# Neighbourhood attention: projections one step sooner, three input blocks on chip, the second block's keys copied apart from its queries

## The reference

```python
qkv = (x @ qkv_w + qkv_b).reshape(B, H, W, 3, HEADS, HEAD_DIM)
q = qkv[..., 0, :, :] * HEAD_DIM ** (-0.5)
kwin = kk[:, idx_h[:, None, :, None], idx_w[None, :, None, :]]      # 7 x 7 keys of each token
vwin = v[:, idx_h[:, None, :, None], idx_w[None, :, None, :]]
scores = jnp.einsum('bxyhd,bxyklhd->bxyhkl', q, kwin) + bias[None]
attn = jax.nn.softmax(scores.reshape(B, H, W, HEADS, k * k), axis=-1)
out = jnp.einsum('bxyhkl,bxyklhd->bxyhd', attn, vwin).reshape(B, H, W, C)
attn_out = out @ proj_w + proj_b
gate = sigmoid(relu(x @ g1_w + g1_b) @ g2_w + g2_b)
return attn_out * gate + x
```

## Time and profile before

| | us |
|---|---|
| median of 3 runs | 4253.98 |
| the profiled execution's own time | 4251.54 |
| its span, from the first to the last instruction | 4249.4 |
| PE busy in it | 3954.3 (93%) |
| DVE busy | 3166.3 (75%) |
| ACT busy | 2744.4 (65%) |
| POOL busy | 1219.7 (29%) |

### The profile page before, as it was taken

How to read it: one execution, slowest core, us unless ns; L and a number is a source line. 1 busy time by engine, 2 the same in 40 slices (tenths; PEclk the granted TensorE clock), 3 DMA queues, 4 the chain that set the end, 5 groups by cost and what they waited for, 6 DMA issues and landing times. The chain is left out here.

```text
span 4249.4 us, 73556 instructions
## 1 busy us (share of the span) xinstructions
PE 3954.3 (93%) x25466; PEld 3038.4 (72%) x25466; DVE 3166.3 (75%) x7667; ACT 2744.4 (65%) x6175; POOL 1219.7 (29%) x1283
## 2 busy tenths in 40 slices
PE   7899997899999999999999999978799987889899
PEld 5677776699988989889988899966566642333247
DVE  5777776677787777877778777759466668887775
ACT  4667766677777777767777667649434447776643
POOL 2444443100011000110001000015124448886753
PEclk8899998899999999999999999999899985887789
DMA  6655554000011000100001000032233345554446
GB/s 176 167 153 158 155 153 114 4 26 21 21 31 33 18 26 16 36 29 23 21 19 42 15 11 9 11 87 75 91 135 119 114 147 180 173 170 154 145 158 208
DMA packets 284396, 365.84 MB, mean 86 GB/s; under 512 B 38650, under 2 KB 169722, under 8 KB 283258
## 3 DMA queue, kind: packets, MB, share of 16 engines
q1 hardware_dynamic: 270154, 343.83, 26.7%
q0 software_dynamic: 12288, 16.92, 1.4%
q10 hardware_dynamic: 1584, 0.40, 0.0%
HBM read 192.80 MB, written 115.34 MB: 73 GB/s over the span
## 5 line engine op out<-in xcount | busy, mean ns | idle before, releaser
L911 ACT ACTIVATE l_ph<-l_T 128x512 fp32r<-128x512 f32 x1024 | 611.8, 597 | 549.2 <-PE l_T L816 549.2
L1028 DVE TENSOR_TENSOR l_pl<-l_T,l_ph 128x512 fp32r<-128x512 f32 x1024 | 707.2, 691 | 275.1 <-ACT l_ph L911 274.4
L1017 DVE CUSTOM_DVE_ANT_0 l_pr<-l_S,l_zero 128x512 f32<-128x512 f32 x1024 | 704.6, 688 | 75.1 <-PE l_S L739 12.1
L916 ACT ACTIVATE l_pr<-l_pr,l_st 128x512 f32<-128x512 f32 x1024 | 731.4, 714 | 1.1 <-DVE l_st L1023 1.0
L828 PE MATMUL l_O<-l_ph,l_vh 128*128 128x256 f32 x2048 | 661.8, 323 | 12.1 <-DVE l_pl L1028 12.0
L816 PE MATMUL l_T<-l_ident,l_pr 128*128 128x128 f32 x4096 | 613.0, 272 | 0.0
L816 PEld LDWEIGHTS l_T<-l_ident,l_pr 128*128 128x128 f32 x4096 | 507.8, 140 | 136.2 <-issue 0.2
L829 PE MATMUL l_O<-l_ph,l_vl 128*128 128x256 f32 x2048 | 577.9, 282 | 0.0
L830 PE MATMUL l_O<-l_pl,l_vh 128*128 128x256 f32 x2048 | 576.2, 281 | 0.0
L1060 POOL TENSOR_TENSOR l_xs<-l_xs,l_bob 128x128 f32<-128x128 f32 x128 | 57.2, 459 | 1643.1 <-DMA l_xs<-x 1641.7
L737 PE MATMUL l_S<-l_kh,l_qh 128*128 128x512 f32 x1024 | 417.6, 408 | 0.3 <-DVE l_kl L977 0.2
(11 more groups left out here) (259 smaller groups left out, 8235.0 us busy)
## 6 DMA issues: line engine op xcount, KB each, us to landing
l3b_u<-ub SPq DMA_DIRECT2D x128, 512.0 KB, 4.0
l_kq<-l_hl SPq DMA_DIRECT2D x384, 128.0 KB, 3.2
zs<-l_tmp SPq DMA_DIRECT2D x64, 256.0 KB, 2.2
ub<-l3a_u SPq DMA_DIRECT2D x32, 512.0 KB, 3.2
l3b_z<-zs SPq DMA_DIRECT2D x64, 256.0 KB, 3.6
yz<-l3b_z SPq DMA_DIRECT2D x64, 256.0 KB, 3.2
l3b_dt<-yz SPq DMA_DIRECT2D x32, 512.0 KB, 4.2
l_vg<-vs SPq DMA_DIRECT2D x256, 55.0 KB
```

The costliest lines, as they stand in the source:

```text
L911: e.activation(ph[:, i, :], psT[:, i, :], ACT.Copy).then_inc(p_hi, 1)
L916: e.activation(pr[:, s, es], pr[:, s, es], ACT.Exp, bias=st[:, s, 9:10], scale=SC, accum_out=st[:, s, 10 + k:11 + k]).then_inc(exped, 1)
L1017: e.tensor_tensor_reduce(pr[:, s, ks], psS[:, bk, :], zero[:].broadcast_to([128, 512]), 1.0, -3.0e38, ALU.add, ALU.max, st[:, s, kc:kc + 1 ...
L1028: e.tensor_tensor(pl[:, i, :], psT[:, i, :], f32(ph[:, i, :]), ALU.subtract).then_inc(p_lo, 1)
```

## The change

The jobs of each block are done one step sooner: step 4(G-2)-1 for "k", then "q", "v" and "hide" in 4(G-2) to 4(G-2)+2. For this `xn` gets a third slot and its semaphores, and ("k", 2) joins the list ahead of the loop. `stack` can copy keys or queries alone: for block 1 the 12 key copies stay where they were, and 12 further copies of its queries, with a semaphore of their own (`q1_in`), stand behind the stores of the first values; scores of block 1 wait for both. The bias classes 3 to 5 are loaded in step 1 instead of 2, and 6 to 8 one each in the steps 14, 18 and 22 instead of together in step 12. The last two pieces of the diff are the wait of PE ahead of the scores of block 1 and that of ACT before it writes `hl` again for block 3.

```diff
-        xn = P.sb("xn", [128, 2, 512])
+        xn = P.sb("xn", [128, 3, 512])
...
+        q1_in = P.sem("q1_in")
...
         def jobs(n):
-            G, i = n // 4 + 2, n % 4
+            G, i = (n + 1) // 4 + 2, (n + 1) % 4
             return [(("k", "q", "v", "hide")[i], G)] if G < NB else []
...
-        before = [("q", 0), ("k", 0), ("k", 1), ("v", 0), ("q", 1), ("v", 1), ("hide", 0), ("open", 0), ("hide", 1), ("open", 1)]
+        before = [("q", 0), ("k", 0), ("k", 1), ("v", 0), ("q", 1), ("v", 1), ("hide", 0), ("open", 0), ("hide", 1), ("open", 1), ("k", 2)]
...
             def fetch(G):
-                s, sl = G % 2, slice(512 * rb, 512 * rb + 512)
-                if G >= 2:
+                s, sl = G % 3, slice(512 * rb, 512 * rb + 512)
+                if G >= 3:
                     for what in ("k", "q", "v", "hide"):
-                        full(w, (what, G - 2))
+                        full(w, (what, G - 3))
...
-            def stack(G):
+            def stack(G, what=("q", "k"), landed=None):
-                for what in ("q", "k"):
-                    emptied(w, (what, G))
+                for x in what:
+                    emptied(w, (x, G))
...
+                to = slice(q_at if "q" in what else k_at, k_at + 1 if "k" in what else q_at + 1, k_at - q_at)
                 for h in range(4):
                     hs = slice(32 * h, 32 * h + 32)
-                    for k, which in enumerate((slice(0, 3, 2), slice(1, 3), slice(0, 4, 3))):
-                        e.dma_start(f32(kq[32 * k:32 * k + 32, h, q_at:k_at + 1:k_at - q_at, :]), f32(halves[hs, which, :])).then_inc(kq_in[G % 4], 16)
+                    for k, (q_part, k_part) in enumerate(((0, 2), (1, 2), (0, 3))):
+                        part = slice(q_part if "q" in what else k_part, k_part + 1 if "k" in what else q_part + 1, k_part - q_part)
+                        e.dma_start(f32(kq[32 * k:32 * k + 32, h, to, :]), f32(halves[hs, part, :])).then_inc(landed or kq_in[G % 4], 16)
...
-            fetch(0)
-            fetch(1)
+            for G in range(3):
+                fetch(G)
...
             stack(0)
-            stack(1)
-            fetch(2)
+            stack(1, ("k",))
             keep_v(0)
             keep_v(1)
+            stack(1, ("q",), q1_in)
             fetch(3)
...
-                if n == 2:
+                if n == 1:
                     for k in range(3, 6):
                         bias(k)
-                elif n == 12:
-                    for k in range(6, 9):
-                        bias(k)
+                elif n in (14, 18, 22):
+                    bias(6 + (n - 14) // 4)
...
+                if G == 1:
+                    w.wait_ge(q1_in, 192)
...
+                    if G == 3:
+                        w.wait_ge(q1_in, 192)
```

More of the change, by code:

```diff
@@ L113, in layer0 @@
         first, weights, bias_in = P.sem("first"), P.sem("weights"), P.slots("bias_in", 9)
-        xn_in, kq_in, v_out = P.slots("xn_in", 2), P.slots("kq_in", 4), P.slots("v_out", 4)
+        xn_in, kq_in, v_out = P.slots("xn_in", 3), P.slots("kq_in", 4), P.slots("v_out", 4)
+        q1_in = P.sem("q1_in")
         vg_in, xs_in, y_out = P.slots("vg_in", 5), P.slots("xs_in", 7), P.slots("y_out", 3)
@@ L290, in project @@
             def project(what, G):
-                s = G % 2
+                s = G % 3
                 if (what, G) in early:
@@ L298, in project @@
                 if what in ("q", "k"):
-                    w.wait_ge(xn_in[s], 16 * (G // 2 + 1))
+                    w.wait_ge(xn_in[s], 16 * (G // 3 + 1))
                     w.wait_ge(prepared, 3)
```

## The result

| | before | after |
|---|---|---|
| median of 4 runs, us | 4253.19 (4249.57 to 4263.62) | 4179.83 (4178.84 to 4181.70) |
| the profiled execution's own time | 4251.54 | 4181.70 |
| its span | 4249.4 | 4179.6 |
| last matmul of layer 0 in it | 721.07 | 653.32 |

The ratio of the changed kernel to the one before is 0.9824, with a 95% interval of 0.9806 to 0.9842: 1.8% faster. The forecast was 4172, range 4161 to 4210. Of the 69.8 us that the span lost, 67.8 lie in layer 0 up to its last matmul. The 2.0 behind it are in layers that no kernel here changes: that part took between 3525.7 and 3534.5 us in the ten profiles of this study, so 2.0 us of it say nothing.

A forecast was written before the change was run, and what follows sets the result against it. SP's 21.6 us loop was taken to bound layer 0, making PE wait beside its own 18.5. From 4251.54, minus 81.8 for the period, plus 0.3 for the start, gave 4170.0; the median, 2.4 above, 4172, range 4161 to 4210.

The forecast's parts named there:

- The mechanism: Layer 0: PE waits for copies because SP's queue loops in 21.6 us beside PE's own 18.5.
- The period: Layer 0, tile 8 to tile 120: a block falls from 21.57 to 18.65 us, 81.8 us over 28 blocks.
- The wait for values: SP's queue: waiting for stored values to land falls from 2.44 to about 0.15 us a block.
- SP's slack of 3.9: Copies ahead of PE's score: 3.9 us to spare where 1.1 were lacking, so PE doesn't wait if SP lags no more.
- the clock: Sign: PE's clock over the layer 0 stretch is 0.97 or more of full speed, from 0.93.
- the two waits: Signs: PE's wait for copies falls from 50 us, SP's for values from 61, each to under 10.
- The start: Layer 0 up to tile 8: added copies covered by PE's 3.77 us wait; cost +0.3 us, ends -1 and +7.8.
- Values landing late: Rival: stores land later under denser traffic, 1.5 us of SP's wait stays, period 19.8; 4204 us, chance 0.13.
- Issuing: Rival: SP's 12 copies always take 9.1 us to issue, period 19.2; 4188 us, chance 0.13.
- no gain: Rival: copies are late from their own landing under load, SP's loop closes again at 21.5; 4254 us, chance 0.04.
- slower: Rival: 12 added copies at the start delay the first tiles by 7.8 us, period stays; 4262 us, chance 0.05.

The follow-up runs named there:

- the kernel that keeps step: Changed kernel with each tile's third window load issued from GpSimd instead of SP, and block 1's key and query copies issued together: 4163.39 us.
- block 1 whole: Changed kernel with block 1's copies as 12 of keys and queries together instead of 12 and 12: 4175.85 us.
- the store later: Changed kernel with the store of a block's values one step later in SP's queue, behind the third group of window loads: 4238.46 us.

## Why the prediction was right, and where it was not

**The mechanism** held: PE waited for copies because SP's queue was a loop of 21.6 us, of which 2.4 were a wait for a store just issued. Both edits that matter, the room behind the store and the room for the copies, were tried apart (20.93 and 20.65) and only give 19.07 together.

**The period** is the term that was mis-sized: 18.65 forecast, 19.07 measured, 28 x 0.42 = 12 of the 82 us. The forecast had SP at 18.46 a block, just below PE's 18.50; SP needed 18.36 + 0.70 = 19.06. Its issuing part was right (18.31 against 18.36), its waits were not:

- The wait for values was put at 0.15, since the cover of 3.3 was as long as the median landing; the landing was 3.7 in the changed kernel, and 0.44 stayed.
- SP's waits for PE and DVE, 0.8 a block before, were left out of the 18.46 without a reason. They shrank to 0.26 and didn't vanish.

The forecast then added 0.15 for the two engines waiting for each other, because "SP's slack of 3.9 takes up most of that". Slack evens out long and short blocks only as long as the queue needs no more per block than PE. At 19.06 against 18.50 it is used up: SP was only about 0.5 us out of step at 164.52 (5.4 us behind its projection, against the 4.8 of the kernel that keeps step) and 9.4 behind at 242.66, and then PE waited. So the period was SP's own. What PE lost against 28 x 18.50, 16 us, was 9 of waiting in these blocks and 7 of time at the lower clock. The Trainium skill's fixed cost of about 2.0 us ("DMA: Bandwidth & Descriptors", "Anatomy of one DMA — SWDGE (gpsimd) path"; with it an estimate of 2.6 us for this store) would have let the wait for values vanish, and was further off than the trace's 3.3: the changed kernel's median is 3.7.

**Markers.** Of those named, the clock (0.99) and tile 8 (79.10 for 78 to 79) came as said or nearly so; the period (19.06 by SP's copies for 18.4 to 18.9), the two waits (11.4 and 12.2 us for under 10) and tile 120 (613 for 601) missed. Period and tile 120 missed by this one term, and the waits are what it consists of.

**The start** gave the right number for an incomplete reason. Tile 8 was forecast 0.3 later than before and came 0.6 later; tile 1 waited for its bias as said (until 40.78 for 42 to 43), tile 4 came at 59.36 for 57.0. The sum set the 12 added copies against the kernel before, and called them covered by the wait at tile 8. The run with block 1 whole shows what this hid: without them the same wait ends 8 us sooner. There the store of block 2's values goes out 2.4 us sooner than before (48.41 for 50.77), and the copies of block 3 start 11.3 behind it instead of 16.6, since loads of windows and input now stand in the time that the store takes to land. These two make 7.6 us, and the 12 copies take 7.6 us to issue. Two terms of the change cancelled, and the copies were a real price, not a covered one. That the bias classes 3 to 5 go out in step 1 instead of 2 was not tried by itself.

**Rivals.** Values landing late (4204) was the right direction with a quarter of its size. Issuing did not slow down: 18.36 us a block at a share of 0.66. The other two, no gain and slower, fell with the result itself: SP's loop closed at 19.06 and tile 8 was 0.6 us late.

**The tail** lost 1.6 us that the forecast didn't have: from tile 120 to the last matmul 40.3 us for 38.7 before. It is time at the lower clock behind the last wait for copies. PE waited 3.05 us ahead of tile 120 in the changed kernel, 1.15 before, and 0.56 or nothing in the kernels with block 1 whole. The windows from tile 120's gate matmul to the last matmuls of the changed kernel, the kernel before and the one with block 1 whole, with the granted clock at 0.91, 0.96 and 1.00:

```profile
613.40:653.40 40.00, 38.91 (x535) 32.94 (x534) 31.96 (x126) 30.49 (x102) 19.33 (x33) 0.91 0.25 71
```

```profile
682.70:721.10 38.40, 37.32 (x535) 31.57 (x534) 31.89 (x126) 30.49 (x102) 19.34 (x33) 0.96 0.26 72
```

```profile
609.70:646.60 36.90, 35.85 (x534) 30.16 (x533) 31.48 (x126) 30.35 (x102) 19.79 (x34) 1.00 0.28 80
```

From 613.60 to 620.40 the changed kernel's PE ran at a granted clock of 0.50, its lower level of 1.2 GHz. SP doesn't hold the tail: its last window loads wait for PE, 0.6 to 1.4 us at a time.

**Luck.** The four misses of the profiled time are the period (+11.8), the start (+0.3), the tail (+1.6) and the layers behind (-2.0), 11.7 us in all: 4181.70 for 4170.0. The median came closer, 4179.83 for 4172, because the forecast put it 2.4 above the profiled execution, as before, and it lay 1.9 below it this time. That was luck.

## What to carry to other kernels

A DMA queue in program order is an engine: add up its issues and waits over one period and compare them with the busiest engine's. Here SP issued for 18.4 us beside a PE that is busy for 18.5. Moving SP's waits and the projections together was worth 2.5 us a block, and moving four issues to a queue with time to spare another 0.5, while the busy shares of the engines said nothing of it. A wait for a transfer that stands right behind its issue costs nearly the whole landing; put other issues of the queue between them, more than the median landing takes.

Slack between two loops is a stock that can be used up. It covers single long blocks while the feeding loop needs less per period than the loop it feeds, all its waits counted. When it needs more, here 0.56 us a block in the mean, the slack is used up (4 us within four blocks in the stretch shown), and from then on the slower loop sets the period. So when two demands come out within a few per cent of each other, count every wait of the feeding loop before calling one of them the limit. And what delays the busiest engine ahead of the loop is paid to the end, since that engine has no time to catch up.

## What the runs showed of the hardware

- The store of 256 KB to DRAM landed in a median of 3.3 us in the kernel before, where in most blocks nothing is issued behind it until it has landed, and in 3.5 to 3.8 in the other kernels of this study, even in those with hardly more traffic (3.6 and 3.7 at shares of 0.61 and 0.62). In these another transfer is issued right behind nearly every store. The kernel before has the same difference within itself, from block 3 on: 3.1 in the median of the 26 stores with nothing behind them, and 3.5, 3.7 and 3.8 for the three at an image's end with window loads behind them. Against it, three stores of the kernel with the store later had nothing right behind them and took 4.0 to 4.3. So the cause stays open.
- The cost of issuing on SP hardly depends on what a copy carries: at the start 12 copies of 64 KB took 7.56 us (27.85 in the changed kernel), 12 of 128 KB 7.76 (35.56 with block 1 whole). Behind 1.8 MB of bias loads the 12 took 10.70.
- Short waits of PE cost more than their length. With the store later PE waited 40.3 us for copies up to tile 120, and the 28 blocks took 68 us more than 28 x 18.50; the granted clock of the stretch was 0.94. A wait of 3.05 us in the changed kernel was followed by 6.8 us at the lower level, and cost the tail about 3 us beside its own length (40.3 us against 37.3 with block 1 whole).
